# Self-attention in a decoder layer: softmax denominators inverted as one 128x16 block laid out by DMA, and four score slots in every step

## The reference

```
qkv = layernorm(x) @ w_qkv.T            # 16 heads of 32 columns, sequence 2048, batch 2
scores = q @ k.T / sqrt(32)             # per head 2048 x 2048, no mask
attn = softmax(scores) @ v              # the reference does it by blocks of 512 keys, with a running log-sum-exp
x = x + attn @ w_out.T
# then cross-attention to a context of 154 rows, a shared and a routed feed-forward
```

## Time and profile before

| what | value |
|---|---|
| median of 3 runs | 3310.52 us (3309.83 to 3311.77) |
| the profiled execution | 3310.81 us |
| its span, first to last instruction | 3309.0 us |
| mean granted clock of PE | 0.94 of 2.4 GHz |
| PE, DVE, ACT, POOL busy | 91%, 66%, 49%, 52% of the span |
| self-attention | from about 330 to 2150 us of the span |

### The profile page before, as it was taken

One profiled execution on the slowest core, in us unless ns is written; L12 is line 12 of the kernel. 1 busy time (PEld: TensorE's weight loads), 2 busy tenths in 40 slices (PEclk: granted clock), 3 DMA queues, 4 the chain that ended last, 5 costly groups with the idle time before them and its releaser, 6 DMA issues. The chain is left out here.

```text
span 3309.0 us, 41856 instructions
## 1 busy us (share of the span) xinstructions
PE 3018.6 (91%) x15214; PEld 1726.3 (52%) x15214; DVE 2198.7 (66%) x3919; ACT 1623.4 (49%) x2965; POOL 1725.8 (52%) x697
## 2 busy tenths in 40 slices
PE   8998799999999999999999999789579995889488
PEld 5787344444444444444444444268454553777433
DVE  4331888888888888888888888255348694666323
ACT  2222166666666666666666667522136572222111
POOL 0000288888787878787878788800112001333255
PEclk9999599999999999999999999889878797999689
DMA  7444744744646446446374444269655243333621
GB/s 232 179 167 154 178 102 87 156 91 104 143 104 142 102 99 144 105 106 137 87 156 86 106 120 98 62 196 251 153 141 155 79 120 112 127 142 113 210 79 36
DMA packets 171933, 426.85 MB, mean 129 GB/s; under 512 B 19393, under 2 KB 40802, under 8 KB 151716
## 3 DMA queue, kind: packets, MB, share of 16 engines
q1 hardware_dynamic: 147614, 279.59, 28.9%
q0 software_dynamic: 24128, 144.75, 20.8%
HBM read 172.29 MB, written 126.67 MB: 90 GB/s over the span
## 5 line engine op out<-in xcount | busy, mean ns | idle before, releaser
L778 DVE TENSOR_REDUCE part_max<-ps_s 128x1 f32<-128x512 f32 x2048 | 1270.9, 680 | 305.4 <-PE ps_s L679 305.4
L880 ACT ACTIVATE probs<-ps_st 128x512 f32<-128x512 f32 x2048 | 1086.2, 600 | 548.3 <-PE ps_st L698 526.6
L637 POOL TENSOR_TENSOR added<-added,probs 128x2048 f32<-128x2048 f32 x256 | 1185.6, 4631 | 90.4 <-ACT probs L880 63.5
L679 PE MATMUL ps_s<-k_stack,q_stack 96*128 96x512 f32 x2048 | 841.4, 427 | 28.1 <-POOL max_parts L627 20.7
L698 PE MATMUL ps_st<-q_stack,k_stack 98*128 98x512 f32 x2048 | 861.2, 426 | 5.2 <-ACT probs L880 3.9
L698 PEld LDWEIGHTS ps_st<-q_stack,k_stack 98*128 98x128 f32 x2048 | 388.3, 190 | 508.9 <-ACT probs L880 358.8
L709 PE MATMUL ps_pv<-probs,v_sb 128*32 128x512 f32 x4096 | 549.3, 608 | 0.0
L679 PEld LDWEIGHTS ps_s<-k_stack,q_stack 96*128 96x128 f32 x2048 | 395.0, 193 | 214.5 <-DVE part_max L778 143.8
L645 POOL DMA_DIRECT2D probs<-probs x128 | 111.5, 871 | 230.3 <-PE ps_pv L709 219.2
L1366 PE MATMUL xps_s<-xks_stack,xq_stack 99*128 99x154 f32 (+1 forms) x512 | 122.8, 319 | 55.7 <-DVE xident_r L1479 48.8
L637 POOL TENSOR_TENSOR added<-probs 128x2048 f32<-128x2048 f32 x32 | 146.4, 4575 | 47.2 <-ACT probs L880 47.2
(11 more groups left out here) (266 smaller groups left out, 3567.0 us busy)
## 6 DMA issues: line engine op xcount, KB each, us to landing
probs<-probs POOLq DMA_DIRECT2D x128, 1024.0 KB, 7.0
xq_stack<-q_parts SPq DMA_DIRECT2D x64, 384.0 KB, 4.5
q_stack<-q_hi SPq DMA_DIRECT2D x64, 256.0 KB, 6.3
k_stack<-k_hi SPq DMA_DIRECT2D x64, 256.0 KB, 8.7
q_parts<-q_h_out SPq DMA_DIRECT2D x64, 256.0 KB, 4.9
x_in<-in_x_rows SPq DMA_DIRECT2D x8, 1024.0 KB, 7.0
q_hi<-qk_h_out SPq DMA_DIRECT2D x8, 1024.0 KB, 4.3
q_lo<-qk_l_out SPq DMA_DIRECT2D x8, 1024.0 KB, 6.3
```

What stands on the lines that cost most here:

```text
L637: pool.tensor_tensor(added[:, w % 2], left, probs[:, k % RING], ALU.add).then_inc(added_up, 1)
L679: pe.matmul(ps_s[:, place % BANKS], q_stack[0:ROWS, w % 4, j, t * P:(t + 1) * P], k_stack[0:ROWS, w // BPB, j, n * BLK:(n + 1) * BLK], sta ...
L778: dve.tensor_reduce(part_max[:, s:s + 1], ps_s[:, (w * SLOTS + s) % BANKS], AX.X, ALU.max)\
L880: act.activation(probs[:, k % RING, j], ps_st[:, n % BANKS], ACT.Exp, scale=SCALE).then_inc(item_used, 1)
```

## The change

DVE no longer inverts 128x512 elements of which 32 partitions each hold the same row. ACT copies `ps_d` to SBUF (`dens_out`, after the exponentials of the body's step 4), SP stores one row of each head to DRAM (`dens_rows`, 4 x 512), reads it back as 128 partitions x 16 (`dens_c`), DVE inverts that (`invert`, in front of the first slot of step 7, INVERT_AT), SP stores it (`recip_rows`) and spreads it with four DMAs over 32 partitions each into `attn_out`; POOL multiplies with `attn_raw` (`product`, between its fifth and sixth addition, PRODUCT_AFTER). The last unit is still done by DVE from `ps_d`. SLOTS_AT becomes four in each step.

```diff
-    SLOTS_AT = [4, 4, 4, 4, 3, 3, 2, 4, 5, 5, 5, 5, 4, 4, 0, 0]
+    SLOTS_AT = [4] * 14 + [0, 0]
+    INVERT_AT = 7
+    PRODUCT_AFTER = 4
 # SP
                 def store(i, w):
-                    sp.wait_ge(normalized, at(i, w, 1, 1))
+                    if ends(i, w):
+                        sp.wait_ge(last_normalized, 1)
+                    else:
+                        sp.wait_ge(dens_copied, unit + 1)
+                        sp.dma_start(dens_rows, dens_sb[0:P:HD]).then_inc(dens_moved, 16)
+                        sp.wait_ge(dens_moved, 16 * (unit + 1))
+                        sp.dma_start(dens_c[:], dens_rows.rearrange("j (c e) -> (j c) e", e=HEADS * BLK // P))\
+                          .then_inc(dens_laid, 16)
+                        sp.wait_ge(inverted, unit + 1)
+                        sp.dma_start(recip_rows.rearrange("j (c e) -> (j c) e", e=HEADS * BLK // P), recip_c[:])\
+                          .then_inc(recip_moved, 16)
...
+                        sp.wait_ge(recip_moved, 16 * (unit + 1))
+                        for j in range(HEADS):
+                            sp.dma_start(attn_out[j * HD:(j + 1) * HD, w % 2], recip_rows[j].partition_broadcast(HD))\
+                              .then_inc(recip_loaded, 16)
+                        sp.wait_ge(normalized, unit + 1)
 # POOL
+                def product(i, w):
+                    unit = i * UPB + w
+                    pool.wait_ge(raw_done, unit + 1)
+                    pool.wait_ge(recip_loaded, 16 * HEADS * (unit + 1))
+                    pool.tensor_tensor(attn_out[:, w % 2], attn_out[:, w % 2], attn_raw[:, w % 2], ALU.mult).then_inc(normalized, 1)
...
                         for n in range(4, ADDS):
                             add(i, w, n)
+                            if n == PRODUCT_AFTER and not begins(i, w):
+                                product(*unit_before(i, w))
 # PE, before the totals of step 8
-                            pe.wait_ge(normalized, at(i, w, 1, 0))
+                            pe.wait_ge(dens_copied, at(i, w, 1, 0))
 # DVE
-                def invert(i, w, q):
-                    cols = slice(q * P, (q + 1) * P)
+                def invert(i, w):
+                    unit = i * UPB + w
+                    dve.wait_ge(dens_laid, 16 * (unit + 1))
+                    dve.reciprocal(recip_c[:], dens_c[:]).then_inc(inverted, 1)
+
+                def normalize_last(i, w):
                     dve.wait_ge(dens_done, at(i, w, 1, 1))
-                    dve.reciprocal(ps_d[:, cols], ps_d[:, cols]).then_inc(inverted, 1)
...
+                    dve.reciprocal(ps_d[:], ps_d[:]).then_inc(last_inverted, 1)
...
-                                if not begins(i, w) and FREED <= s < FREED + TPB:
-                                    invert(*ended, s - FREED)
+                                if not begins(i, w) and s == SLOTS_OF[INVERT_AT][0]:
+                                    invert(*ended)
                                 slot_max(*one, s)
-                                if not begins(i, w) and s == FREED + TPB - 1:
-                                    normalize(*ended)
 # ACT
+                def dens_out(i, w):
+                    unit = i * UPB + w
+                    act.wait_ge(dens_done, unit + 1)
+                    if unit:
+                        act.wait_ge(dens_moved, 16 * unit)
+                    act.activation(dens_sb[:], ps_d[:], ACT.Copy).then_inc(dens_copied, 1)
...
+                            if k == LATE + 1 and not begins(i, w):
+                                dens_out(*unit_before(i, w))
```

More of the change, by code:

```diff
@@ L438, in _, with self_attention @@
                 blocks(pe, body)
-def self_attention(nc, q_hi, q_lo, k_hi, k_lo, v_rows, eye, attn_t, k_stack, v_sb, wo_t, wq_t, next_w, next_raw, next_h, next_l, next_a):
+def self_attention(nc, q_hi, q_lo, k_hi, k_lo, v_rows, eye, attn_t, k_stack, v_sb, wo_t, wq_t, next_w, next_raw, next_h, next_l, next_a,
+                   dens_rows, recip_rows):
     HEADS = 4
@@ L483, in self_attention @@
         attn_raw = sb("attn_raw", [P, 2, BLK])
+        dens_sb = sb("dens_sb", [P, BLK])
+        dens_c = sb("dens_c", [P, HEADS * BLK // P])
+        recip_c = sb("recip_c", [P, HEADS * BLK // P])
         attn_out = sb("attn_out", [P, 2, BLK])
@@ L499, in self_attention @@
         raw_done, inverted, normalized = sem("raw_done"), sem("inverted"), sem("normalized")
+        dens_copied, dens_moved, dens_laid, recip_moved, recip_loaded = (
+            sem(n) for n in ("dens_copied", "dens_moved", "dens_laid", "recip_moved", "recip_loaded"))
+        last_inverted, last_normalized = sem("last_inverted"), sem("last_normalized")
         out_stored = [sem(f"out_stored{s}") for s in range(2)]
@@ L550, in self_attention, with ends @@
         SLOTS_OF = list(slots_of())
-        FREED = SLOTS_OF[LATE + 1][1]
+        def ends(i, w):
+            return isinstance(i, int) and i == TURNS - 1 and w == UPB - 1
         q_units = [s.rearrange("b (g j r) (n k) -> b g n r j k", g=QUADS, j=HEADS, n=BPB) for s in (q_hi, q_lo)]
@@ L579, in store @@
                 def store(i, w):
-                    sp.wait_ge(normalized, at(i, w, 1, 1))
                     unit = i * UPB + w
+                    if ends(i, w):
[9 more added lines that the diff above has]
+                          .then_inc(recip_moved, 16)
+                        if unit >= 2:
+                            sp.wait_ge(out_stored[w % 2], 16 * (unit // 2))
+                        sp.wait_ge(recip_moved, 16 * (unit + 1))
[3 more added lines that the diff above has]
+                        sp.wait_ge(normalized, unit + 1)
                     b, g = unit // (QUADS * BPB), unit % (QUADS * BPB) // BPB
@@ L798, in max_rows @@
                     dve.tensor_reduce(parts[:, :, :, 1], max_rest[:].unsqueeze(3), AX.X, ALU.max).then_inc(parts_done, 1)
-                def invert(i, w, q):
-                    cols = slice(q * P, (q + 1) * P)
+                def invert(i, w):
[3 more added lines that the diff above has]
+                def normalize_last(i, w):
                     dve.wait_ge(dens_done, at(i, w, 1, 1))
-                    dve.reciprocal(ps_d[:, cols], ps_d[:, cols]).then_inc(inverted, 1)
-                def normalize(i, w):
+                    dve.reciprocal(ps_d[:], ps_d[:]).then_inc(last_inverted, 1)
+                    dve.wait_ge(out_stored[w % 2], 16 * ((i * UPB + w) // 2))
                     dve.wait_ge(raw_done, at(i, w, 1, 1))
[L807 to L810, removed]
+                    dve.wait_ge(last_inverted, 1)
+                    dve.tensor_tensor(attn_out[:, w % 2], ps_d[:], attn_raw[:, w % 2], ALU.mult).then_inc(last_normalized, 1)
                 def body(i, last):
@@ L836, in body @@
                     if last:
-                        for n in (UPB - 2, UPB - 1):
-                            for q in range(TPB):
-                                invert(i, n, q)
-                            normalize(i, n)
+                        normalize_last(i, UPB - 1)
                 dve.wait_ge(ident_loaded, 16)
```

3 lines of the change are left out of this document (2 added, 1 removed).

## The result

The changed kernel takes 3276.22 us (median of 4 runs, 3273.78 to 3279.23) against 3310.18 for the kernel before beside it (4 runs, 3308.95 to 3311.77): ratio 0.9898, 95% interval 0.988 to 0.9915. That is 34 us faster where 5.5 was forecast. The time lies in the range and the sign is right, but a large part of the sum is not, and three of the six loading units were shorter than 55 us, which the prediction had named as a sign of being wrong.

A forecast was written before the change was run, and what follows sets the result against it. PE was taken to set the pace. Six loading units at +6.1 us (+37), twenty-four ordinary ones at -1.85 (-44.5) and the end (+2) gave -5.5, so 3305 us; range 3257 to 3344.

The forecast's parts named there:

- The table and the relief: Ordinary units: four slots everywhere, without DVE's four inversions and product, save 1.96 us each; late second links cost 0.1.
- ACT's copy and the small DMAs in ordinary units: Copy costs nothing; the two DMAs take 2.2 and 2.0 us, landing 18.7 into a unit with 2.5 slack.
- the rival of late units everywhere: Lay-out in ordinary units takes longer or collides with the first link: at 4 us per DMA, 3341 us; chance 0.16.
- Free passage: Loading units: small transfers do not suffer behind v, the lay-out lands by 21.2; -51, 3259 us; chance 0.13.
- The first small DMA behind v: Loading units: issued at 14.45, it comes in at 22, 5.4 late; the second is issued at 22.1.
- The stall of 7 us: Loading units: the second small DMA's pieces go one by one until the link ends, about 28.1; PE stops 22.0 to 29.0.
- My last rival: The same as the rival of late units everywhere; it has the first link issued 1.5 us later than before.
- The rival of the one turn: Loading units: first small DMA held behind v, second goes in one turn; stall 3.5, +2.7 each, 3284 us; chance 0.17.
- The clock: Loading units: the gap drops PE to 1.2 GHz, back within about 5 us, losing 2.2; bounds 1 and 8.6.
- The forecast's terms for loading units: Six units, 4, 8, 12, 16, 20 and 24, in which k and v load: +6.1 us each, +37.
- The end: Last units: PE waits for POOL's additions in unit 31, so product time and part of unit 30's saving are lost: +2.

The follow-up runs named there:

- the table alone: The kernel before with four slots in every step and nothing else: 3375.37 us, ratio 1.0193.
- the relief alone: The changed kernel with the old slot table: 3359.74 us, ratio 1.0156; with v's load also moved behind the ended unit's store: 3314.3 us, 1.0011.
- the product of 4 columns: The changed kernel with POOL's product working on 4 of its 512 columns: 3292.62 us, ratio 0.9964.
- The kernel with v behind the store: The changed kernel with the load of v issued after the ended unit's store instead of before it: 3250.32 us, ratio 0.9814.
- the last-product kernel: The changed kernel with v's load behind the store and, in the last unit, POOL's product behind its last addition: 3251.26 us, ratio 0.9831.

## Why the prediction was right in sign and far off in size

- **The table and the relief** (-1.96 and +0.1 each): confirmed. Steps 8, 10 and 11 are 3.07 apart and undisturbed units take 52.1; the mean ordinary unit lost 1.73 us, since late second links cost some 0.3 and not 0.1; 24 of them give -41.5 where I had -44.5. How the credit is shared the other kernels say: the table alone costs 2%, the relief alone gives nothing (1.0011), both give -1.9%, the last two with v out of the way. The relief alone is worth 0.7 us in an undisturbed unit (54.1 to 53.4) and the table on top of it 1.3 (to 52.1); without the relief the same table costs 2 us a unit.
- **ACT's copy and the small DMAs in ordinary units**: confirmed. The first small DMA takes 1.7 us and the second 1.6 (I had 2.2 and 2.0), the inversion runs at 20.5 without a wait (I had 20.6). So the rival of late units everywhere falls. Free passage falls too, since the first small DMA is held behind v.
- **The first small DMA behind v**: confirmed; the second is issued 21.2 to 22.5 us into a loading unit where I had 22.1, and moving v takes it back to 17.2 to 18.1. The rest, up from 15.9, is k's, which I had not looked at.
- **The stall of 7 us**: this step failed. I let the second small DMA meet a link "just issued" at 21.1 and had the pieces dealt out one for one. The stall was 1.5 to 2.8 us. The mechanism is real and its size was right: the relief alone and the product of 4 columns show gaps of 7 to 8.7 us on DVE and of 6.2 to 7.8 on PE. What was wrong is the time of the link. I took 21.1 from unit 4 of the kernel before, where POOL issues the first link at 7.5; in the change POOL's product stands in front of it. My last rival even named this delay, 1.5 us, for ordinary units, but the sum for the loading units leaves it out. The link comes at 8.8, the second by that at 21.2 to 22.1 in loading units, and the small DMA, issued from 0.45 us before it to 0.35 after it, passes. That it does so is luck: 0.2 us more in the unit with the narrowest margin would have turned it. The rival of the one turn came nearest (3284 us, with +2.7 for a loading unit where +0.8 was measured), though not for its reason: the pieces pass by being there first, and once behind they are dealt out or held. The rule of the Trainium skill, "DMA: Bandwidth & Descriptors", section "Queues, rings and completion order", by which an engine typically takes 9 to 17 descriptors from one queue before it turns to the next, would give the bunch of 144 above too (9 for each engine), but not the 91 to 90 packets behind a link, which are one for one.
- **The clock**: I charged 2.2 us in each loading unit. Three of six stood at the lower clock for 3.4, 10.2 and 6.8 us and lost 9 us in all by it, instead of 13 in six, and three lost nothing. The forecast's terms for loading units, 37 us, came out as 4.7.
- **The end** (+2): -0.2. PE does wait longer there, 13.54 us instead of the 7.63 of the earlier trace rows, since its unit is shorter and POOL is not, yet the whole from unit 30 on takes no longer than before.
- **Not forecast**: 4.9 us more in the later stages, where no instruction was changed. The granted clock is 0.87 in this part in both traces. The kernel with v behind the store has the very same later stages, and there this part took 1149.5 us, against 1156.4 in the change and 1151.5 before. So executions differ here by more than the 4.9, and nothing shows that it is the change's.

Together -41.5 + 4.7 - 0.2 + 4.9 = -32.1, the 32.3 us of the profiled executions.

## What to carry to other kernels

A kernel's own times of issue may not be used for a change that adds work in front of the issuing instruction: here 1.3 us of work on POOL moved a link by 1.1 to 1.3 us once the units had become too short for POOL to be idle there, which turned a race of half a microsecond and kept four stalls of 7 us away. Where two transfers meet, work out which one is there first, and give both outcomes a price; a result that hangs on such a race is better made safe, as by loading v behind what is urgent. The inversion taken from DVE gave nothing on the whole until the order of the work around it was changed too, and the order alone was worth less than nothing: try such edits together.

## What the runs showed of the hardware that was not expected

- 128 pieces of 64 bytes issued up to 0.5 us after an accumulating DMA of 1 MB go through ahead of it in 1.5 to 1.7 us; issued 0.6 us or more after it they take 5.3 to 6.5 us, until it is nearly through.
- Where a load of 16 KB of instructions came among the last packets of such a DMA (26.1 to 26.9 us into a unit), it landed 0.2 to 0.9 us later than the usual 6.9 after its issue; with the old table, where small pieces of another DMA were dealt out in it or came at its end as well, 2.1 to 2.5 us later than 7.0 in six of seven cases. That is a coincidence which no run took apart, and it is not the only cause: in two units of the last-product kernel (1 and 29) the link took 8.1 and 7.8 us beside a load of only 8 KB.
- The same length of idle time on PE, 1.7 us, was followed by the lower clock for 6.8 us in one unit (20) and by none in another (12). With the table alone it fell in 17 units although PE never stood idle for more than 0.7 us at once in front of it.
